# A graph network kernel: counts above a limit gathered in 17 pieces over three rounds, and their products placed within the banks

## The reference

```python
# layer 2: three rounds of propagation
norm = _gcn_norm(edge_index, edge_weight, num_nodes)      # per edge
for _ in range(NUM_LAYERS):                               # 3
    agg = segment_sum(norm[:, None] * out[row], col)
    out = clip(agg * ALPHA + res, 0.0, 1.0)
...
# layer 3: three rounds, each with a batch norm; the weight of an edge is 1
for i in range(N_LAYERS):                                 # 3
    z = segment_sum(wn[:, None] * z[src], dst)
    z = relu(z)
    z = _batchnorm(z, gammas[i], betas[i])
```

## Time and profile before

| | |
|---|---|
| median of 3 runs | 3460.56 us (3457.35 to 3468.86) |
| span of the profiled execution, first to last instruction | 3465.3 us |
| its own time | not listed apart from the three times above |
| mean granted TensorE clock | 0.943 of full speed |
| DMA in the span | 388.67 MB, 112 GB/s on average |
| TensorE / VectorE / ScalarE / POOL busy | 2974.6 / 2742.9 / 2280.7 / 2141.3 us |
| propagation round 1, products to turned sums | 3147.2 to 3212.8 us |
| propagation round 2, the same | 3217.3 to 3305.6 us |
| opening count round, first product to last sum | 3318.2 to 3367.1 us |

### The profile page before, as it was taken

The page is one execution under the profiler, slowest core; times in us unless marked ns, Lnnn a source line. Parts: engine busy times, 40 slices in busy tenths (PEclk is TensorE's granted clock), DMA queues, the critical chain, the costliest instruction groups (busy, mean ns, idle before and its releaser), DMA issues. The chain is left out here.

```text
span 3465.3 us, 69301 instructions
## 1 busy us (share of the span) xinstructions
PE 2974.6 (86%) x19703; PEld 2370.4 (68%) x19703; DVE 2742.9 (79%) x6018; ACT 2280.7 (66%) x3192; POOL 2141.3 (62%) x1629
## 2 busy tenths in 40 slices
PE   3888788988856999999999999999999976657657
PEld 3677677777745888888888888888888851113257
DVE  6678988888856999999999999999999973441065
ACT  3678688888836888888888888888888842220000
POOL 4048888888877777777777777777777730000000
PEclk9899899999977999999999999999999997798778
DMA  9943222222222333333333333333333359998940
GB/s 400 419 154 38 12 15 15 15 16 16 15 25 41 53 53 52 50 53 51 50 53 51 50 53 51 51 53 52 50 53 52 50 187 426 426 391 342 373 172 6
DMA packets 265695, 388.67 MB, mean 112 GB/s; under 512 B 149903, under 2 KB 200838, under 8 KB 259254
## 3 DMA queue, kind: packets, MB, share of 16 engines
q0 software_dynamic: 149184, 120.78, 20.7%
q1 hardware_dynamic: 100034, 195.42, 16.6%
q10 hardware_dynamic: 16416, 71.74, 5.1%
HBM read 260.01 MB, written 127.78 MB: 112 GB/s over the span
## 5 line engine op out<-in xcount | busy, mean ns | idle before, releaser
L585 POOL DMA_INDIRECT both<-kept x782 | 1333.0, 1705 | 439.8 <-issue 194.6
L923 PEld LDWEIGHTS ps<-prod,big 128*128 128x128 f32 x7840 | 1133.9, 190 | 137.7 <-DVE prod L1290 133.0
L923 PE MATMUL ps<-prod,big 128*128 128x170 f32 x7840 | 1183.2, 310 | 22.5 <-DVE prod L1290 17.4
L593 POOL DMA_INDIRECT kept<-feat_dram,kept x782 | 760.8, 973 | 243.2 <-issue 233.1
L668 ACT ACTIVATE big<-iota_b,kept 128x640 f32<-128x640 f32 x1029 | 779.0, 815 | 13.6
L914 PE MATMUL ps<-prod,onehot 128*128 128x320 f32 x3920 | 684.5, 325 | 81.2 <-DVE prod L1320 79.6
L914 PEld LDWEIGHTS ps<-prod,onehot 128*128 128x128 f32 x3920 | 597.7, 194 | 112.9 <-DVE prod L1320 84.5
L673 ACT ACTIVATE big<-big 128x2560 f32<-128x2560 f32 x196 | 458.0, 2337 | 277.2 <-PE ps L923 277.1
L988 PE MATMUL ps<-w2mix,kept 65*128 65x384 f32 x1568 | 559.3, 500 | 21.7 <-ACT kept L720 20.4
L1462 DVE TENSOR_REDUCE kept<-kept 128x80 f32<-128x1280 f32 x392 | 561.4, 1471 | 0.0
L988 PEld LDWEIGHTS ps<-w2mix,kept 65*128 65x128 f32 x1568 | 284.2, 191 | 179.7 <-issue 25.5
(11 more groups left out here) (235 smaller groups left out, 3028.9 us busy)
## 6 DMA issues: line engine op xcount, KB each, us to landing
both<-big POOLq DMA_DIRECT2D x40, 1910.0 KB, 91.2
big<-both SPq DMA_DIRECT2D x24, 1600.0 KB, 11.8
big<-both SPq DMA_DIRECT2D x24, 1528.0 KB, 13.2
kept<-keys_dram SPq DMA_DIRECT2D x196, 128.0 KB, 3.0
kept<-in_wT SPq DMA_DIRECT2D x196, 128.0 KB
adj_c<-kept ACTq DMA_DIRECT2D x42, 400.0 KB, 31.6
kept<-adj_c SPq DMA_DIRECT2D x9, 1600.0 KB, 22.4
adj_w<-kept ACTq DMA_DIRECT2D x16, 800.0 KB, 33.6
```

Of the source, the lines that this page charges most:

```text
L585: pool.indirect_dma_start(both, bass.IndirectOffsetOnAxis(ap=sc_idx[:, c:c + 1], axis=0), sc_val[:, c // 2, c % 2, :], None, compute_op=AL ...
L593: pool.indirect_dma_start(gath[:, s % 2, k, :], None, feat_dram, bass.IndirectOffsetOnAxis(ap=src_i[:, 4 * s + k:4 * s + k + 1], axis=0)). ...
L923: mm = pe.matmul(part_sums(part, MSG), onehot[:, q, k, part * P:(part + 1) * P], prod[:, q, k, 0:HI * MSG], start=False, stop=False, skip_ ...
```

## The change

Flagging the heavy rows stays where it was. Numbering them (`find_slots`) comes after group 0 of round 1, and finding their node numbers (`find_rows`) is cut into three sets of 12, 12 and 1 blocks, after groups 1, 2 and 3 of round 1. The picks for that are written three times into a small place in `both_tmp`; the full `picks` are written again after `split_z`, at their old place. The rows are gathered in 17 pieces of 184 columns; VectorE converts pieces 0 to 3 in round 1 and 4 to 11 in round 2, each before it copies the round's sums, and 12 to 16 after the picks. As `over16` lies in `big`, which the rounds use for weights, a converted piece is stored to a new DRAM tensor `over_dram` by POOL, and SP loads the whole once all 17 pieces and the padding are stored. In the opening round `add_over` now follows within each bank, as in the later rounds, and TensorE waits for that load in the first bank.

```diff
-EIGHTH = TCOLS // 8
+PIECES = 17
+PIECE = TCOLS // PIECES
+PIECES_BY_ROUND = (0, 4, 12, PIECES)
+PICK_SETS = ((0, 12), (12, 24), (24, NA))
...
+        over_dram = nc.dram_tensor("over_dram", [P, NP], F16, kind="Internal").ap()
...
+        few_picks = both_tmp[:, 0:12 * P // 2].bitcast(BF16).rearrange("p (a k) -> p a k", a=12)
+        over_in = [prod_all[:, NP:NP + 2 * PIECE], iota_b[:, 80:80 + 2 * PIECE]]
+        over_out = iota_b[:, 80 + 2 * PIECE:80 + 3 * PIECE].bitcast(F16).rearrange("p (q n) -> p q n", q=2)
...
 # sync
+                    sp.wait_ge(s_overpad, 16)
+                    for q in range(2):
+                        sp.wait_ge(s_overout[q], 16 * len(range(q, PIECES, 2)))
+                    sp.dma_start(over16, over_dram).then_inc(s_over16, 16)
...
 # gpsimd
             pool.wait_ge(s_ridx, 1)
-            for e in range(8):
-                if e >= 2:
-                    pool.wait_ge(s_over, e - 1)
-                pool.indirect_dma_start(over_in[:, e % 2, :], None, eighths,
-                                        bass.IndirectOffsetOnAxis(ap=row_idx[:, e:e + 1], axis=0),
-                                        ).then_inc(s_overin[e % 2], 16)
+            pool.dma_start(over_dram[:, TCOLS:NP], zero_bf[:, 0:NP - TCOLS].bitcast(F16)).then_inc(s_overpad, 16)
+            for e in range(PIECES + 1):
+                if e < PIECES:
+                    if e >= 2:
+                        pool.wait_ge(s_over, e - 1)
+                    pool.indirect_dma_start(over_in[e % 2], None, pieces,
+                                            bass.IndirectOffsetOnAxis(ap=row_idx[:, e:e + 1], axis=0),
+                                            ).then_inc(s_overin[e % 2], 16)
+                if e >= 1:
+                    pool.wait_ge(s_over, e)
+                    pool.dma_start(over_dram[:, (e - 1) * PIECE:e * PIECE],
+                                   over_out[:, (e - 1) % 2, :]).then_inc(s_overout[(e - 1) % 2], 16)
...
 # tensor, spmm_round
                     group(k, (3 * k, 3 * k + 1, 3 * k + 2))
+                    if r == 1 and k == 0:
+                        find_slots()
+                    elif r == 1 and k <= len(PICK_SETS):
+                        find_rows(k - 1)
...
 # tensor, count_round
-                    if opening and s == 7:
-                        find_rows()
                 pe.wait_ge(s_z, r * 3 - 3)
+                if opening:
+                    pe.wait_ge(s_picks, 1)
...
-                    if not opening:
-                        if b == 0:
-                            pe.wait_ge(s_zcc, r - 2)
-                        add_over(b)
-                if opening:
-                    pe.wait_ge(s_zcc, 1)
-                    pe.wait_ge(s_over, 8)
-                    for b in range(BANKS):
-                        add_over(b)
+                    if b == 0:
+                        pe.wait_ge(s_zcc, r - 2)
+                        if opening:
+                            pe.wait_ge(s_over16, 16)
+                    add_over(b)
...
 # vector
+            def heavy_rows():
+
+                dve.wait_ge(s_slot, 1)
+                link(V.scalar_tensor_tensor(out=slot_no[:, :], in0=ps[:, 7, 0:NA], scalar=1.0, in1=flag[:, :],
+                                            op0=ALU.add, op1=ALU.mult))
+                for i, (a0, a1) in enumerate(PICK_SETS):
+                    if i:
+                        dve.wait_ge(s_rowno, i)
+                    picks_of(few_picks[:, 0:a1 - a0, :], a0, a1).then_inc(s_few, 1)
+                dve.wait_ge(s_rowno, len(PICK_SETS))
...
+            def heavy_pieces(e0, e1):
+
+                for e in range(e0, e1):
+                    dve.wait_ge(s_overin[e % 2], 16 * (e // 2 + 1))
...
+                    if e >= 2:
+                        dve.wait_ge(s_overout[e % 2], 16 * (e // 2))
+                    V.tensor_copy(over_out[:, e % 2, :], whole).then_inc(s_over, 1)
...
+                    heavy_rows()
+                if r >= 1:
+                    heavy_pieces(PIECES_BY_ROUND[r - 1], PIECES_BY_ROUND[r])
                 copy_sums(r)
...
-            for e in range(8):
...
+            picks_of(picks, 0, NA).then_inc(s_picks, 1)
+            heavy_pieces(PIECES_BY_ROUND[2], PIECES)
```

More of the change, by code:

```diff
@@ L335, in gnn_program @@
         s_slot = sem("slots_in_psum")
+        s_few = sem("some_picks_ready")
         s_picks = sem("picks_ready")
@@ L339, in gnn_program @@
         s_overin = [sem(f"heavy_part{q}_loaded") for q in range(2)]
-        s_over = sem("overflow_part_ready")
+        s_over = sem("overflow_piece_ready")
+        s_overout = [sem(f"overflow_piece{q}_stored") for q in range(2)]
+        s_overpad = sem("overflow_padding_stored")
+        s_over16 = sem("overflow_part_loaded")
         s_zc = sem("heavy_z_in_psum")
@@ L608, in _ @@
                         add(c)
-            eighths = both[0:TABLE, :].rearrange("(s d) o -> s (d o)", d=EIGHTH)
+            pieces = both[0:TABLE, :].rearrange("(s d) o -> s (d o)", d=PIECE)
             pool.wait_ge(s_ridx, 1)
-            for e in range(8):
-                if e >= 2:
-                    pool.wait_ge(s_over, e - 1)
-                pool.indirect_dma_start(over_in[:, e % 2, :], None, eighths,
-                                        bass.IndirectOffsetOnAxis(ap=row_idx[:, e:e + 1], axis=0),
-                                        ).then_inc(s_overin[e % 2], 16)
+            pool.dma_start(over_dram[:, TCOLS:NP], zero_bf[:, 0:NP - TCOLS].bitcast(F16)).then_inc(s_overpad, 16)
[10 more added lines that the diff above has]
+                                   over_out[:, (e - 1) % 2, :]).then_inc(s_overout[(e - 1) % 2], 16)
         @block.scalar
@@ L1037, in find_slots, with find_rows @@
                 pe.wait_ge(s_flag, 1)
-                pe.matmul(ps[:, 1, 0:NA], earlier[:, :], flag[:, :], start=True, stop=False, skip_group_check=True)
+                pe.matmul(ps[:, 7, 0:NA], earlier[:, :], flag[:, :], start=True, stop=False, skip_group_check=True)
                 for a in range(NA - 1):
-                    mm = pe.matmul(ps[:, 1, a + 1:NA], ones_w[:, :], flag[:, a:a + 1].broadcast_to([P, NA - 1 - a]),
+                    mm = pe.matmul(ps[:, 7, a + 1:NA], ones_w[:, :], flag[:, a:a + 1].broadcast_to([P, NA - 1 - a]),
                                    start=False, stop=True, skip_group_check=True)
                 mm.then_inc(s_slot, 1)
-            def find_rows():
-                pe.wait_ge(s_picks, 1)
-                for a in range(NA):
-                    mm = pe.matmul(ps[:, 6, 0:2], picks[:, a, :], node_ids[:, a, :], start=(a == 0), stop=(a == NA - 1))
+            def find_rows(i):
+                pe.wait_ge(s_few, i + 1)
+                a0, a1 = PICK_SETS[i]
+                for a in range(a0, a1):
+                    mm = pe.matmul(ps[:, 7, 64:66], few_picks[:, a - a0, :], node_ids[:, a, :], start=(a == 0),
+                                   stop=(a == NA - 1), skip_group_check=True)
                 mm.then_inc(s_rowno, 1)
@@ L1508, in copy_sums, with picks_of @@
                 dve.wait_ge(s_turn, r + 1)
+            def picks_of(to, a0, a1):
+                n = a1 - a0
+                return V.tensor_tensor(to.rearrange("p a (t k) -> p a t k", k=SLOTS),
+                                       slot_no[:, a0:a1].unsqueeze(2).unsqueeze(3).broadcast_to([P, n, 2, SLOTS]),
+                                       iota_b[:, 1:SLOTS + 1].unsqueeze(1).unsqueeze(1).broadcast_to([P, n, 2, SLOTS]),
+                                       ALU.is_equal)
+            def heavy_rows():
[7 more added lines that the diff above has]
+                dve.wait_ge(s_rowno, len(PICK_SETS))
+                link(V.tensor_reduce(row_no[:, :], ps[:, 7, 64:66], AX, ALU.add))
+                link(V.tensor_scalar(row_no[:, :], row_no[:, :], float(PIECES), None, ALU.mult))
+                V.tensor_scalar(row_idx[:, :], iota_b[:, 0:PIECES], row_no[:, 0:1], None, ALU.add).then_inc(s_ridx, 1)
+            def heavy_pieces(e0, e1):
+                for e in range(e0, e1):
+                    dve.wait_ge(s_overin[e % 2], 16 * (e // 2 + 1))
+                    got = over_in[e % 2].rearrange("p (n o) -> p n o", o=2)[:, :, 0]
+                    whole = over_in[e % 2].bitcast(I32).rearrange("p (n o) -> p n o", o=2)[:, :, 0]
+                    link(V.tensor_scalar(whole, got, float(CAP), -float(CAP), ALU.max, ALU.add))
+                    V.tensor_scalar(whole[0:SLOTS, :], whole[0:SLOTS, :], 511, None, ALU.bitwise_and)
+                    link(V.tensor_scalar(whole[SLOTS:P, :], whole[SLOTS:P, :], 9, None, ALU.arith_shift_right))
+                    if e >= 2:
+                        dve.wait_ge(s_overout[e % 2], 16 * (e // 2))
+                    V.tensor_copy(over_out[:, e % 2, :], whole).then_inc(s_over, 1)
             link(V.memset(big[:, 1:4:2, 2 * WIDE[1]:NP], 0.0))
```

25 lines of the change are left out of this document (1 added, 24 removed).

## The result

| | before | after |
|---|---|---|
| median (4 runs each, one chip) | 3459.31 us (3457.35 to 3468.86) | 3500.69 us (3496.24 to 3504.81) |
| span of the profiled execution | 3465.3 us | 3499.8 us |
| first copy of round 0's sums | 3131.27 us | 3163.12 us |
| from there to the end | 334.0 us | 336.7 us |

The ratio is 1.0122, 95% interval [1.0105, 1.0140]: 41 us slower by the medians, outside my range of 3456 to 3482. By the last two rows of the table, **31.9 us of the 34.5 by which the profiled execution is longer are already there when the propagation begins**, 24 us ahead of the first instruction that the change adds (`find_slots`, 3187.0), and only 2.7 come up in the part that it rewrites.

The account below looks back on a forecast made before the run. Rounds 1 and 2 were taken as bound by DMA, the opening count round by its chain of overflow gathers and VectorE operations. Tail gain -2 plus transfer loss 10 made +8 us: 3468.6 us, range 3456 to 3482.

Parts of the forecast that it names:

- Part 1: Round 1: finding the rows there costs nothing (up to 1 us without cover), index ready at about 3175.
- Part 2: Rounds 1 and 2: gathers land in 8 us, conversions finish ahead of the copies, tightest in round 1 with 4 us to spare.
- Part 3: Rounds 1 and 2: 11 gathers at 0.65 and 8.5 stores at 0.35 us delay the loads, 10 us lost (6 to 15).
- Part 4: Opening count round: overflow part loaded at 3350, TensorE idle 12 us inside bank 0, gain 2 us (0 to 6).
- the Trainium skill's fit: Tail's store and load: 2.0 us plus bytes over 436 GB/s, part there at about 3346, gain 6 us.
- Rival C: Round 1: gathers land in over 12 us, piece 3 unconverted at its end, copy held; +15 to +28, say +20; chance 0.15.
- Rival D: Opening count round: overflow part in place when TensorE ends bank 0, -10 to -12 us; chance 0.05.

Follow-up runs that it names:

- no_stores: Changed kernel at its old SBUF places without stores, DRAM tensor and load, the part zeroed by one VectorE instruction: 3453.81 us, ratio 0.9984 to before.
- before_1_store_last: Kernel before with one small plain store by POOL behind its last gather: ratio 1.0115 to before, 37.9 us longer.
- the nine: Kernels where POOL issues a transfer to DRAM behind or between its row gathers: shortest add 1541 to 1551 ns, 392nd add at 1075 to 1088 us.
- the eleven: Kernels where POOL issues no transfer to DRAM behind or between its row gathers: shortest add 1538 ns, 392nd add at 1042 to 1066 us.
- shift64: Kernel before with an unused 64-byte tile behind row_idx, so every later SBUF tile lies 64 bytes higher: ratio 0.9993 to before.
- shift32: Kernel before with an unused 32-byte tile there, so all later SBUF tiles lie 32 bytes higher: ratio 1.0006 to before.
- before_longer_streams: Kernel before with 52 small VectorE memsets behind the last eighth and 27 already met waits on POOL ahead of its first gather: ratio 1.0023 to before.
- pieces_on_chip: Changed kernel without stores, DRAM tensor or load: 12 pieces converted in round 2 into h and sq, five in the count round: 3454.24 us, ratio 0.9985 to before.

## Why the prediction was wrong

**The step that failed** is its first sentence: I read the profile "from the end of the scatter phase on, since the change touches nothing before it". That put the change's effect on the scatter phase at nothing, with no term in the sum. None of the instructions there is changed, and yet 31.9 of the 34.5 us arise there. No rival had it, so the range could not hold it. That the delay belongs to the stores is shown: taken out of the changed kernel they take it along (`no_stores`), added to the kernel before they bring it (`before_1_store_last`), tensor, addresses, streams and number of DMAs are excluded, and stores issued by SP do not bring it. Why a transfer to DRAM behind the gathers lengthens adds that ran 2100 us earlier stays **open**. Two things are measured. In the first layer every kernel of the nine has a shortest add that is 3 to 13 ns longer, and it stays so beyond 980 us (median 1540 ns before, 1544 after); times 392 that is 1 to 5 us, so it is not the delay itself. And the delay grows little with it: against a mean of 1052 us in the eleven, the 392nd add comes at 1076 to 1084 with 3 ns, 1081 to 1086 with 5, 1087 with 13. In the second layer the mean add is as long as before. That a slightly later add meets VectorE's instructions differently is my guess; nothing here shows it, nor what makes the 3 ns, nor why the second layer is spared.

The rest of the working, against the means of `before`, `shift64`, `shift32` and the eight other kernels whose names begin with `before` (70.5 us in round 1, 93.1 in round 2 and, without `before_longer_streams`, 170.0 for the rest; these eleven are not the eleven without the delay). Among them round 1 differs by up to 1.5 us and round 2 by up to 3.5, so the smaller differences below are estimates:

- **Part 1**, finding the rows in round 1 at no cost. The index came at 3207.8, or 3175.9 with the 31.9 taken off: forecast 3175. Round 1 of `pieces_on_chip`, which finds the rows, converts nothing in it and gathers only two pieces (at 3162.7 and 3164.0), took 72.4 for 70.5. The two gathers account for about 1 us of that, and single kernels of before reach 71.3: what is left for finding the rows is under 1 us, or nothing.
- **Part 2**, the gathers' pace. They landed in 7.2 us, taken as 8; pieces 0 to 3 were converted by 3230.6 (3198.7; forecast 3197), 4 to 11 by 3284.7 (3252.8; forecast 3255), and the copy of round 1 was released by TensorE with 6.27 us to spare.
- **Part 3**, what the transfers take. Round 1 lost 3.3 us in the three kernels with the change's pieces at their places (forecast 4), round 2 lost 4.9 (forecast 6). The split is read from `no_stores`: with gathers alone 3.1 and 2.3 (mean of its two kernels). So 11 gathers cost 5.4 us, 0.49 each for my 0.65 and the 0.45 of their bytes: here the bytes were the better guide. Stores cost nothing measurable in round 1 and 2.6 us for eight in round 2, 0.33 each for my 0.35. That is three times the 0.11 of their bytes; whether their rows, being under 512 bytes, have a part in it, no run separates.
- **Part 4**, the tail. TensorE's wait ended at 3386.39, 28.7 us behind the first product, forecast 31.8: store and load took 1.83 and 4.10 us, where I took 5 and 5.3, while the last piece was ready 22.6 us behind the first product, 1.1 later than I had it. The gain was 3.9 to 4.9 us for my 2, and the idle time 9.4 for 12; the lower clock cost 2.3 us, forecast 1.9. Here the Trainium skill's fit ("DMA: Bandwidth & Descriptors", Anatomy of one DMA), 2.1 and 3.9 us, was the better estimate, though the page gives it for POOL's path and the load is issued by SP; its 6 us of gain were 1 to 2 too many. The error was mine: the 6.1 us of POOL's small store had 40 stores of 1.9 MB right behind it, while the store of the last piece had no other beside it.

Against each other, parts 3 and 4 make 3.3 us, with a forecast of 8. Rival C did not occur: no conversion was late. Rival D wanted the part in place at the end of bank 0; the two kernels without stores, which do not add the part, come near it (a mean rest of 156.7 for 170.0), and of the 13.4 us that they win there the rounds take back 5.4.

That the total lies above my range is thus due to the scatter phase alone: the parts that the forecast of +8 us spoke of made 3.3, inside its bounds of 0 to +15. The median of 3500.69 less the 31.9 of the profile is 3468.8, next to my 3468.6, and that is luck: the parts were off by more, and medians and profiled spans do not differ by the same (41.4 and 34.5 us).

## What to carry to other kernels

Compare where a changed kernel's phases begin before you explain its total: one look at the start of the first touched phase tells how much of the total the touched part can explain at all. In this kernel a phase in which POOL's DMAs run beside a busy VectorE answered to program text far from it, so time the whole program, and try transfers on another queue or none: intermediate results that fit into bytes which are dead for one round need no trip through DRAM. Moving transfers into a stage that is bound by DMA costs at least their bytes (0.49 us a gather for 0.45, 0.33 a store for 0.11); it pays only if what is taken off the path is longer.

## What was not expected of the hardware

- One plain store issued by POOL behind its last gather made the whole kernel 37.9 us longer (ratio 1.0115 [1.0098, 1.0133]); a store ahead of those gathers cost 2.3 us (ratio 1.0013 [0.9995, 1.0030]), and 27 of them from the sync engine 0.8.
- The delay hits the first layer's 392 adds and not the second's, whose mean is 1626 ns before and 1625 after.
- The shortest scatter-add of the first layer fell into four values, by program: 1538 ns in eleven, 1541 in three, 1543 in five, 1551 in one (one profile of each).
- Beside loads that fill the DMA engines a store of 128 rows of 368 bytes lengthened round 2 by an estimated 0.33 us, and alone it landed in 1.83 us, a load of 0.8 MB behind it in 4.10.
- From one comparison to another the median of the kernel before went from 3449.14 to 3472.06 us, and its single runs within one spread over some 20 (3446.38 to 3468.63). The 392nd add of the eleven kernels, 1042.5 to 1065.8, spreads as widely, so the same stretch may make it; single executions without a profile cannot show that.
